# DLRM interaction and top MLP on one core: Gram products of two samples at a time, fewer one-hot lookups in the second pair of tiles, and a hand-written order for the last blocks

## The reference, cut to what matters

```
e = jnp.stack([tbl_0[ids[:, 0]], ..., tbl_25[ids[:, 25]]], axis=1)
all_emb = jnp.concatenate([bottom_output[:, None, :], e], axis=1)     # [2048, 27, 128]
gram = jnp.einsum('bfd,bgd->bfg', all_emb, all_emb)
z = gram[:, _TRIU_I, _TRIU_J]                                         # 351 pairs
h = jnp.concatenate([z, r_bottom_output], axis=1)
h = jnp.maximum(h @ W_top1 + b_top1, 0.0)                             # 479 -> 512
h = jnp.maximum(h @ W_top2 + b_top2, 0.0)                             # 512 -> 256
y = h @ W_top3                                                        # 256 -> 1
```

## Time and profile before

| what | before |
|---|---|
| median of 3 runs | 382.97 us (382.36 to 384.99) |
| the profiled execution | 382.43 us, its span in the profile 380.7 us |
| TensorE busy | 348.3 us (91%) |
| DVE busy | 261.8 us (69%) |
| ACT busy | 117.8 us (31%) |
| POOL busy (issuing gathers) | 263.8 us (69%), until 349 us |
| chain that ended last | PE 80%, DVE 15%, DMA 3% |

### The profile page before, as it was taken

How to read it: one execution, slowest core, us unless ns; L and a number is a source line. 1 busy time by engine, 2 the same in 40 slices (tenths; PEclk the granted TensorE clock), 3 DMA queues, 4 the chain that set the end, 5 groups by cost and what they waited for, 6 DMA issues and landing times.

```text
span 380.7 us, 14045 instructions
## 1 busy us (share of the span) xinstructions
PE 348.3 (91%) x6112; PEld 311.4 (82%) x6112; DVE 261.8 (69%) x781; ACT 117.8 (31%) x218; POOL 263.8 (69%) x281
## 2 busy tenths in 40 slices
PE   0879869999998999989998999989999899999997
PEld 0767759898887999978887898978998799887886
DVE  4999998985757957566537866677767586723232
ACT  3453641333223322313232341313323133132311
POOL 5777777777777777777777777777777777775000
PEclk9999998999999999999999999999999899999999
DMA  7755574332242312212331322413123212121000
GB/s 229 198 148 205 173 236 163 94 85 55 54 97 58 92 51 57 79 50 59 98 92 50 94 54 54 106 51 91 50 58 99 57 50 57 52 57 46 4 2 1
DMA packets 16684, 32.42 MB, mean 85 GB/s; under 512 B 5488, under 2 KB 8176, under 8 KB 16496
## 3 DMA queue, kind: packets, MB, share of 16 engines
q0 software_dynamic: 8704, 17.84, 18.4%
q1 hardware_dynamic: 7920, 13.69, 11.6%
HBM read 31.50 MB, written 0.01 MB: 83 GB/s over the span
## 4 chain that ended last, share of the span: by engine, by line
PE 80%; DVE 15%; DMA 3%; issue 1%; ACT 1%; SPq 0%; ACTq 0%; DVEq 0%
PE hot_ps L366 36%; DVE onehot L496 11%; PE gram_ps L346 11%; PE h_ps L407 10%; PE h_ps L419 8%; PE xt_ps L329 7%; PE h_ps L404 5%; DVE tab L545 3%; DMA stage_sb<-in_hot_dram 3%; PE zt_ps L385 2%; DVE h L535 1%; PE hot_ps L407 0%; ACT tab L633 0%; DMA ids_wide<-in_hot_ids_dram 0%; DVE Z L504 0%
## 5 line engine op out<-in xcount | busy, mean ns | idle before, releaser
L318 POOL DMA_INDIRECT X<-in_table_dram,rows_sb x272 | 262.4, 965 | 84.3 <-issue 81.1
L496 DVE TENSOR_SCALAR onehot<-ids_wide,row_value 128x256 fp32r<-128x256 int16 x640 | 199.5, 379 | 81.4 <-PE hot_ps L366 78.5
L366 PE MATMUL hot_ps<-onehot,tab 128*128 128x256 f32 x1280 | 191.9, 298 | 13.7 <-DVE onehot L496 13.5
L366 PEld LDWEIGHTS hot_ps<-onehot,tab 128*128 128x128 f32 x1280 | 166.7, 194 | 20.4 <-issue 13.3
L475 ACT COPY XT<-xt_ps 128x512 f32<-128x512 f32 x64 | 38.9, 608 | 165.2 <-PE xt_ps L329 165.2
L346 PEld LDWEIGHTS gram_ps<-XT 128*27 128x27 f32 x4096 | 40.6, 105 | 23.1 <-issue 14.8
L346 PE MATMUL gram_ps<-XT 128*27 128x26 f32 x4096 | 53.5, 190 | 4.4 <-DVE Z L504 3.2
L604 ACT COPY XT<-hot_ps 128x256 f32<-128x256 f32 x72 | 49.4, 686 | 25.1 <-PE hot_ps L366 24.7
L407 PE MATMUL h_ps<-stage_sb,w_sb 128*128 128x256 f32 (+3 forms) x198 | 45.1, 363 | 0.0
L329 PE MATMUL xt_ps<-ident,X 128*128 128x128 f32 x272 | 40.8, 272 | 2.1 <-ACT XT L471 1.9
L419 PE MATMUL h_ps<-w_sb,stage_sb 128*128 128x256 f32 x128 | 32.9, 402 | 9.3 <-DVE h L535 9.3
(11 more groups left out here) (32 smaller groups left out, 59.6 us busy)
## 6 DMA issues: line engine op xcount, KB each, us to landing
ids_wide<-in_hot_ids_dram SPq DMA_DIRECT2D x14, 320.0 KB
X<-in_table_dram,rows_sb POOLq DMA_INDIRECT x272
stage_sb<-in_hot_dram SPq DMA_DIRECT2D x15, 256.0 KB, 4.2
stage_sb<-in_hot_dram SPq DMA_DIRECT2D x10, 192.0 KB, 3.1
bottomT<-in_bottom_t_dram SPq DMA_DIRECT2D x8, 128.0 KB, 4.1
w_sb<-in_w_dram SPq DMA_DIRECT2D x1, 1024.0 KB
w_sb<-in_w_dram SPq DMA_DIRECT2D x1, 512.0 KB, 9.2
vec_sb<-in_vecs_dram SPq DMA_DIRECT2D x1, 256.0 KB, 9.3
```

Source lines behind the costliest of these rows:

```text
L318: pool.indirect_dma_start(X[:, n % RING, k, :], None, table, bass.IndirectOffsetOnAxis(idx[:, column:column + 1], 0)).then_inc(gathered[n ...
L366: mm = pe.matmul(hot_ps[i % 2][:, 0:WIDE], tab[u][:, part, D * c:D * (c + 1)], onehot[p % ONEHOTS][:, c - PIECE[u][h], :], start=(c == 0 a ...
L496: compared = dve.tensor_scalar(onehot[p % ONEHOTS][:, c - PIECE[u][h], :], ids_wide[:, u, :], row_value[:, c:c + 1], None, ALU.is_equal)
```

## The change

The core of the diff, with all that the sections below speak of:

```
-RING = 7
+RING = 5
-ONEHOTS = 5
+ONEHOTS = 3
+PAIR = 2
+SPLIT_STEPS = 6
+HALF_ROWS = PAIR * PAD
+GROUPS_PER_BLOCK = PAD // 4
-HOTS = [HOT_BASE, HOT, HOT, HOT, HOT_BASE, HOT, HOT, HOT]
+HOTS = [HOT_BASE, HOT_BASE, HOT, HOT, HOT_BASE, HOT, HOT, HOT]
...
-        XT = sb("XT", [P, XTILES, P, SLOTS])
+        XT = sb("XT", [P, XTILES, P, PAD])
+        gram_sb = sb("gram_sb", [P, NG, PAD])
...
-            def gram(b, run):
+            def gram(b):
                 t, j = b // BLOCKS, b % BLOCKS
+                pe.wait_ge(xt_moved, UNITS_OF[b][-1] + 1)
...
+                wait(pe, gram_kept, b - 1)
+                for k in range(PAD // PAIR):
+                    pos, rows, at = PAD * j + PAIR * k, HALF_ROWS * (k % 2), PAIR * NG * (k // 2)
+                    pair = XT[:, t % XTILES, pos:pos + PAIR, :]
+                    mm = pe.matmul(gram_ps[rows:rows + HALF_ROWS, b % 2, at:at + PAIR * NG],
+                                   pair.rearrange("d s f -> d (s f)"), pair[:, :, 1:SLOTS], start=True, stop=True)
+                mm.then_inc(gram_full, 1)
...
             def step(b):
-                for n in UNITS_OF.get(b + 1, [])[:-1]:
+                units = UNITS_OF.get(b + 1, [])
+                for n in units[:-1]:
                     transposes(n)
-                lookup_run(b, 0)
-                for n in UNITS_OF.get(b + 1, [])[-1:]:
+                lookup_slice(b)
+                gram(b)
+                for n in units[-1:]:
                     transposes(n)
-                gram(b, 0)
-                for run in range(1, RUNS):
-                    lookup_run(b, run)
-                    gram(b, run)
                 mlp(b // BLOCKS, b % BLOCKS)
+
+            def last_step(b):
...
+                if b == TILES * BLOCKS - BLOCKS + 2:
+                    gram_block(b)
+                    layer1(len(JOBS) - 2, 0)
+                    layer1(len(JOBS) - 2, 1)
+                    next_units(b)
+                    layer1(len(JOBS) - 2, 2)
+                    layer1(len(JOBS) - 2, 3)
+                    layer2(TILES - 3)
+                if b == TILES * BLOCKS - 1:
+                    layer2(TILES - 2)
+                    gram_block(b)
...
+        def keep_gram(eng, copy, b, quadrants):
+            t, j = b // BLOCKS, b % BLOCKS
+            eng.wait_ge(gram_full, b + 1)
+            wait(eng, z_ready, t)
+            for q in quadrants:
+                rows = slice(PAD * q, PAD * (q + 1))
+                mine = slice(NG * (q % PAIR), NG * (q % PAIR + 1))
+                kept = copy(gram_sb[rows, :, GROUPS_PER_BLOCK * j:GROUPS_PER_BLOCK * (j + 1)].rearrange("p n g -> p g n"),
+                            gram_ps[rows, b % 2, 0:GROUPS_PER_BLOCK * PAIR * NG
+                                    ].rearrange("p (g n) -> p g n", n=PAIR * NG)[:, :, mine])
+            kept.then_inc(gram_kept, 1)
...
             def z_transpose(t):
-                dve.wait_ge(gram_full, BLOCKS * (t + 1))
+                dve.wait_ge(gram_kept, BLOCKS * (t + 1) + (1 if t == TILES - 1 else 0))
                 wait(dve, folded_all, t)
-                dve.transpose(Z[:].rearrange("p g (b m) -> p g b m", b=2),
-                              gram_ps[:, :, 0:NG * GROUPS_PER_BANK].rearrange("p b (m g) -> p g b m", g=NG)
+                dve.transpose(Z[:].rearrange("p n m -> p (n m)"), gram_sb[:].rearrange("p n g -> p (n g)")
...
-                for p in pieces_ended(b):
+                freed = pieces_ended(b)
+                for p in freed[:1]:
+                    one_hot(p + ONEHOTS)
+                if t >= 3 and t % 2 == 1 and j == 3 and t < TILES - 1:
+                    layer3(t - 3)
+                if t == TILES - 1 and j >= 2:
+                    layer3(t - 5 + j)
+                for p in freed[1:]:
                     one_hot(p + ONEHOTS)
...
+            keep_gram(dve, nc.vector.tensor_copy, TILES * BLOCKS - 1, (2, 3))
+            layer3(TILES - 2)
             z_transpose(TILES - 1)
...
+                for n in units[-1:]:
+                    move_xt(act, nc.scalar.copy, n)
+                keep_gram(act, nc.scalar.copy, b, (0, 1) if b == TILES * BLOCKS - 1 else (0, 1, 2, 3))
```

More of the change, by code:

```diff
@@ L180, in build @@
         gram_full = sem("gram_full")
+        gram_kept = sem("gram_kept")
         z_ready = sem("z_ready")
@@ L427, in mlp @@
                     z_transposes(t - 1)
-                if t == TILES - 1 and j >= 2:
-                    layer1(len(JOBS) - 2, 2 * (j - 2))
-                    layer1(len(JOBS) - 2, 2 * (j - 2) + 1)
                 if g >= 0:
@@ L456, in _ @@
                     transposes(u - 3)
-            for b in range(TILES * BLOCKS):
+            for b in range(LAST):
                 step(b)
+            for b in range(LAST, TILES * BLOCKS):
+                last_step(b)
             z_transposes(TILES - 1)
-            layer2(TILES - 2)
             for c in range(C1):
@@ L557, in step @@
                     fold(t - 1)
-                if b < SOMETIMES:
-                    u = HOT_BASE + b
-                    for q in range(FIRST_PIECE[u], FIRST_PIECE[u + 1]):
-                        split_second(q)
-                if t >= 3 and t % 2 == 1 and j == 3:
-                    layer3(t - 3)
+                for q in LATE_PIECES[PER_STEP * b:PER_STEP * (b + 1)]:
+                    split_second(q)
                 if t >= 4 and t % 2 == 0 and j == 0:
@@ L593, in _ @@
         def _(act):
-            def moves(b):
-                for n in UNITS_OF.get(b, []):
-                    move_xt(act, nc.scalar.copy, n)
             def place_hot(i):
@@ L647, in step @@
                 relus(t, j)
-                moves(b + 1)
+                if b == TILES * BLOCKS - 2:
+                    relu(len(JOBS) - 2, 0)
+                    relu(len(JOBS) - 2, 1)
+                units = UNITS_OF.get(b + 1, [])
+                for n in units[:-1]:
+                    move_xt(act, nc.scalar.copy, n)
                 for i in ended(b):
```

80 lines of the change are left out of this document (44 added, 36 removed).

## The result

The changed kernel takes 404.48 us (median of 4 runs, 403.35 to 405.53), the kernel before 382.67 us beside it (382.06 to 384.99). The ratio is 1.056, 95% interval 1.050 to 1.0615: slower by about 22 us. The forecast was 397 us, 381 to 413.

A forecast was written before the change was run, and what follows sets the result against it. TensorE's own instructions were taken as the bound, with POOL's gathers some 11 us behind. 350.3 us to the last eight blocks, plus 23.6 and 20.9, made a span of 394.8, forecast as 397 us, range 381 to 413.

The forecast's parts named there:

- the forecast's own case: Whole kernel: wider Gram blocks and a longer end make it slower, 386 to 404 us; chance 0.48.
- the growing waits: Rival, tile starts: slower ACT copies and three one-hot pieces make 24 us of waits, not 9.3; 411 us, chance 0.19.
- The wide block: Gram block on TensorE: 0.34 us entry and exit plus 0.89 stream, 1.23 us, 0.16 more than before.
- Columns are free: Rival, Gram stream: a half takes loads every 26.4 ns whatever its width, gathers bound; 382.7 us, no change, chance 0.2.
- No overlap: Rival, Gram stream: the two halves run one after the other, 1.9 us a block, about 450 us; chance 0.08.
- The second pair with six lookups: Early blocks: 80 lookups (9.5 us) go, eight gathers (10.1 us) come; from this alone no gain.
- The copies: ACT after each Gram block: four copies at 0.5 us, 2 us a block, 128 us in all.
- The gap of 4 us behind the last Gram block: TensorE near the end: copies, square transpose and fold, hidden before, now stand uncovered, 4 us idle.
- Block 16: Its transposes at 114.1 us, 0.4 later than before; the gathers allow 113.6, so no gain is left.
- The five pairs: Up to the last eight blocks: 40 x 0.16 us for wider blocks, less 1.4 us net from waits and clock.
- The last eight blocks: From their start to the last unit's transposes: 23.6 us where it was 15.5, with more work ahead.
- the tail: From the last unit's transposes to the end: 20.9 us against 20.3 before, with the fold chain uncovered.

The follow-up runs named there:

- pair1_hot_2: Changed kernel with ten lookups for the second pair of tiles (pair 1) again, so 272 gathers; 405.48 us, ratio 1.059.
- layer3_first: Kernel before, with only `layer3` moved behind the first one-hot refill and ahead of the others; 372.78 us, ratio 0.970.
- tail_order_2: Changed kernel with the last Gram block ahead of two `layer1` blocks and `layer2(14)`, and DVE's fold ahead of `layer3(14)`; 398.17 us, ratio 1.0375.
- unit_behind: Changed kernel with the transposes of a block's first unit, where it has two, behind the slice of lookups; 403.30 us, ratio 1.052.
- z_behind: Changed kernel with DVE's square transpose behind a tile's first one-hot refill, not first in the queue; 401.22 us, ratio 1.045.
- the first four kernels: Changed kernel with narrow products, those plus one ACT copy, ten pair-1 lookups, or another end order, together on one chip: 537.23, 532.80, 489.37, 489.17 us.

## Why the prediction was right, and where it was not

The forecast's span was 394.8 us, the measured one 403.4: 8.6 us short, with the sign and the main mechanism right. The 404.48 us measured lie half a us past the forecast's own case (386 to 404), in the stretch that it had given to the growing waits.

**Right.** *The wide block*: 1.23 us predicted with its entry and exit. Measured are 1.07 from the loads to the transposes. The entry is as before: TensorE's loads stand idle for 0.13 us ahead of the samples in both kernels (210.86 behind 207.94 + 2.79; 208.01 behind 206.50 + 1.38), so with the 0.20 us of the prediction a block takes 1.27, 0.20 more than the 1.07 before. The stream itself was 0.90 (0.89 predicted). *Columns are free*, the first rival, is refuted: a half takes its next load after 2 x 28.1 = 56 ns, not 26.4. The Trainium skill, page "TensorEngine Tiling (Array Packing)", section Performance Considerations, puts a fixed cost of some 60 cycles on each matmul and lets one of a single column last as long as one of 60. The trace disagrees with it for these fp32 products: 56 ns at 52 columns where it was 26.4 at 26. Whether the moving or the stationary columns set the 56 ns is open: both were doubled together. *No overlap* is refuted as well (1.9 us). *The second pair with six lookups* brings nothing in the end (`pair1_hot_2`), and block 8's loads start at 68.01 us, "not before 67.8" as said. *The copies*: 0.521 us for 0.5. *ACT's load* 238 us for 245. *The gap of 4 us behind the last Gram block* is there (4.03).

**Block 16: 114.1 predicted, 120.6 measured, the largest miss.** The failing step is "For block 16 it is the 21st unit: 84 gathers ... Nothing is left of the gain there", followed by adding only 8 x 0.16 + 2 x 0.62 us to 113.67 - 2.1. Gathers and TensorE were treated as two limits of which the later one counts, and no wait was put between blocks 8 and 16. In this stretch the trace shows 5.3 us of waits on TensorE's products where the kernel before has 0.7: 3.0 us in two waits for gathers, 1.5 for one-hots, 0.8 for ACT to empty `hot_ps`. (The third wait for gathers, 2.4 us, lies ahead of block 8.) One of the two, with the work behind it:

```profile
89.10 0.42 PEld L336 LDWEIGHTS xt_ps<-ident,X 128*128 128x128 f32 x4 [2.73 <-DMA X<-in_table_dram,rows_sb]
89.49 4.21 PEld L369 LDWEIGHTS hot_ps<-onehot,tab 128*128 128x128 f32 x23
```

```profile
84.00:94.00 10.00, 7.67 (x57) 6.83 (x55) 2.15 (x8) 3.70 (x7) 7.56 (x9) 0.83 0.31 86
```

The 23 lookups take 4.21 us where 22 took 2.79 at full clock, and the stretch of 10 us at a mean clock of 0.83 holds 10 x 0.17 = 1.7 us lost to the clock, which the prediction left out. Waits (5.3 - 0.7) and clock together are 6.3 us, and the miss is 6.5. `pair1_hot_2`, which waits for no gather and keeps the full clock there, still needs 47.8 us from block 8 to block 16, where the kernel before needs 43.7 and the prediction's terms (8 x 0.16) give 45.0. Of the missing 2.8 us its own waits for one-hots (1.6) and for ACT (0.8) are 1.7 more than the 0.7 before.

**The five pairs: +5.0 predicted, +6.1 measured** (block 16 to block 56: 232.1 us against 226.0). "New waits of between 0 and 24 us ... 9.3, pays back just what the moved `layer3` saves" came out nearly as said, in part by another way: in this stretch lookups wait 5.7 us for one-hots and, which the prediction did not have, 3.1 us for ACT to empty `hot_ps`, 8.8 in all, where `layer2` waited 9.1 us for `layer3` before. Beside `layer3_first`, which has the moved call and nothing else, the five pairs take 232.1 us against 216.4. Of these 15.7 us, 40 wider blocks are 8 (40 x 0.20) and the waits are 7.4 (8.8 against 1.4). So the change costs more than its 22 us show: beside `layer3_first` (372.78 us) the changed kernel is 31.7 us slower, and the moved `layer3` hides a part of that.

**Luck: 2.9 us.** The sum took 350.3 for the start of the last eight blocks from the row at 344.87, the products of block 56. In the kernel before these start 5.2 us behind the block's transposes (339.6), since half a step of lookups and samples lies between. In the new order only `layer2` does, and it is 2.3 us:

```profile
352.71 0.42 PEld L336 LDWEIGHTS xt_ps<-ident,X 128*128 128x128 f32 x4
...
355.03 1.01 PEld L350 LDWEIGHTS gram_ps<-XT 128*64 128x64 f32 x32 [0.33 <-issue]
```

The sum didn't take off the difference, which hides part of the miss at block 16.

**The last eight blocks: 23.6 predicted, 23.9 measured** (355.03 to 378.92); **the tail: 20.9 predicted, 24.5 measured** (from the last unit's loads at 378.92). The failing step is "from the last tile's `layer1` to the end 380.7 - 372.25 = 8.45", which took the end over from a trace in which TensorE had come to it without a pause. With 4 us of idle time ahead the same stretch starts at 392.72 and ends at 403.4: 10.7 us, at half the clock for the first part. In `tail_order_2`, at full clock, it takes 8.3 (387.99 to 396.3). The gap was foreseen, its consequence for the clock was not. `tail_order_2` shows 6.3 us of the loss to be this order's.

**The rival with growing waits** named the right chain (copies, square transpose, refills) and the wrong size: it asked for 24 us of waits, and 8.8 came.

**The parts don't add up to a proof.** Stream 11.8, tail 6.3, square transpose 3.3, first unit 1.2 and pair 1 none are about 22.6 us, near the loss of 22. But `unit_behind` and `z_behind` undo nothing, and their differences lie within the noise or at its edge. The moved `layer3` is a gain inside the change (11.6 us in the kernel before, and 2.7, not clear of the noise, in the changed one), and each kernel ran alone. That the sum meets the loss is chance. A gain on one wait that is read from the kernel before doesn't carry over to a kernel in which the helper engine is late for another reason.

## What to carry to other kernels

Halving the number of products doesn't make them cheaper when each becomes twice as wide and half as many run side by side; take the price from how far apart the loads start, and try it once at the new width, before counting instructions. When two limits lie near each other (here TensorE's work and the gathers), work in front of one of them and waits for the other add up within a stretch, and three waits of 2.6 to 4.0 us looked at here were each followed by work at half the clock, a fourth was not. When a wait seems to be gone from the list of waits, look whether it stands there under another name, as the wait of 9 us in `z_behind`. And look first for a short call that stands behind long ones in a helper engine's queue: moving `layer3` alone, within the kernel before, gave 3%, more than anything else here.

## What the runs showed of the hardware that was not expected

**A chip that starves TensorE.** On the chip of the first four kernels the kernel before takes 530 us instead of 383. TensorE is idle there with no event to end it. These are the waits of the kernel with narrow products, on that chip and then on the other:

```profile
PEld gram_ps L350 <- issue: 115.1, 166, 1.3
```

```profile
PEld gram_ps L350 <- issue: 4.0, 9, 1.0
```

The order of the kernels turns around with it (the changed kernel itself was not run there): with 14045 instructions 530 us, with 14243 and 14052 537 and 533, but with 10314 and 10147 only 489 each (0.92 of the kernel before), although the same two are 6% and 4% slower than the kernel before elsewhere. This fits a chip on which TensorE's instructions arrive slowly, so that fewer and wider products pay. That this is the cause was not tried. A verdict on a change that trades the number of instructions for their width may thus hold for one of the two chips only.

**The clock after short waits.** Waits of 2.6, 2.7 and 4.0 us were each followed by a granted clock of half: 23 lookups in 4.19 and 4.21 us, and a stretch of 6 us at 0.50. It isn't so each time. In `pair1_hot_2` lookups wait 2.7 us for ACT at 57 us, and the clock stays at full:

```profile
PEld hot_ps L369 <- ACT tab L681: 5.0, 4, 2.7
```

```profile
52.00:62.00 10.00, 6.83 (x78) 6.30 (x77) 7.63 (x21) 6.89 (x14) 7.87 (x8) 1.00 0.91 290
```

**Narrow copies are not cheap.** 32 partitions with 208 numbers take 0.521 us on ACT, hardly less than the 0.587 us for 128 partitions with 512 numbers (`move_xt`).
